# Turning the adjacency blocks on VectorE in 32 x 32 blocks, squaring on ScalarE, and partial mixes that stay in their banks

## The reference

```python
h = maximum(layernorm(x), 0)
msg = h @ W0 + B
weights = where(adj < 1, exp(-(1/adj - 1)**2 / (2 * 0.5**2)), 0)   # 0 where adj is 0
x = x + weights @ msg                                             # first layer

h = maximum(layernorm(x), 0)
A = adj + eye
d = sum(A, axis=1) ** -0.5
x = x + relu(d[:, None] * A * d[None, :] @ (h @ W1.T))             # second layer
```

## Time and profile before

| what | value |
|---|---|
| median of 3 runs | 651.94 us (651.78 to 652.38) |
| span of the profiled execution | 651.7 us |
| PE busy | 595.8 us, 91% |
| DVE busy | 523.2 us, 80% |
| ACT busy | 479.0 us, 73% |
| moved by DMA | 157.67 MB, mean 242 GB/s |

### The profile page before, as it was taken

One profiled execution on the slowest core, in us unless ns is written; L12 is line 12 of the kernel. 1 busy time (PEld: TensorE's weight loads), 2 busy tenths in 40 slices (PEclk: granted clock), 3 DMA queues, 4 the chain that ended last, 5 costly groups with the idle time before them and its releaser, 6 DMA issues.

```text
span 651.7 us, 7163 instructions
## 1 busy us (share of the span) xinstructions
PE 595.8 (91%) x2307; PEld 337.1 (52%) x2307; DVE 523.2 (80%) x582; ACT 479.0 (73%) x357; POOL 65.2 (10%) x87
## 2 busy tenths in 40 slices
PE   2498988977979999999999999999999999999995
PEld 2475644544545555655555555554555554444432
DVE  4999999999999999999999994668763868531516
ACT  2799999999999999999999986476484665710000
POOL 2694000000000100010001000100000000001110
PEclk9799999999999999999999999999999999999999
DMA  9987685797886778677678883585744550527983
GB/s 258 388 322 252 236 293 194 263 313 261 271 284 229 253 264 303 252 237 266 223 272 312 300 337 130 186 283 194 268 168 152 202 221 0 205 83 301 301 295 104
DMA packets 54293, 157.67 MB, mean 242 GB/s; under 512 B 2561, under 2 KB 11010, under 8 KB 43778
## 3 DMA queue, kind: packets, MB, share of 16 engines
q1 hardware_dynamic: 48370, 114.43, 50.8%
q0 software_dynamic: 5904, 42.99, 18.0%
HBM read 112.33 MB, written 45.09 MB: 242 GB/s over the span
## 4 chain that ended last, share of the span: by engine, by line
PE 58%; DVE 22%; ACT 8%; issue 8%; DMA 3%; DVEq 0%; SPq 0%; ACTq 0%; POOL 0%; POOLq 0%
PE acc L381 18%; PE acc_late L420 11%; PE acc_once L397 11%; PE turned_ps L364 9%; PE turned_ps L519 6%; DVE rowpart L659 6%; DVE wt L680 5%; DVE wt L673 4%; DMA late<-adj_t_spill 3%; ACT wt L586 2%; PE side L420 2%; ACT wt L580 2%; ACT kept L569 2%; ACT wt L574 2%; DVE msg L779 1%
## 5 line engine op out<-in xcount | busy, mean ns | idle before, releaser
L381 PE MATMUL acc<-wt,msg 128*128 128x512 f32 x512 | 231.8, 596 | 20.4 <-ACT wt L586 20.4
L569 ACT COPY kept<-turned_ps 128x1024 f32<-128x1024 f32 x128 | 124.0, 1027 | 75.5 <-PE turned_ps L364 73.6
L680 DVE SCALAR_TENSOR_TENSOR wt<-wt 128x2048 f32<-128x2048 f32 x64 | 146.3, 2286 | 20.8 <-ACT wt L580 20.7
L381 PEld LDWEIGHTS acc<-wt,msg 128*128 128x128 f32 x512 | 93.8, 190 | 126.9 <-issue 101.9
L659 DVE TENSOR_REDUCE rowpart<-raw 128x4 f32<-128x2048 f32 x64 | 145.8, 2278 | 7.7 <-DMA raw<-in_adj_dram 7.7
L673 DVE SCALAR_TENSOR_TENSOR wt<-kept 128x2048 f32<-128x2048 f32 x64 | 146.2, 2284 | 5.0 <-ACT kept L569 5.0
L364 PEld LDWEIGHTS turned_ps<-ident,raw 128*128 128x128 f32 x1024 | 119.8, 144 | 36.7 <-issue 29.8
L364 PE MATMUL turned_ps<-ident,raw 128*128 128x128 f32 x1024 | 126.9, 279 | 9.6 <-DMA raw<-in_adj_dram 9.4
L586 ACT ACTIVATE wt<-wt 128x2048 f32<-128x2048 f32 x64 | 123.2, 1926 | 15.7 <-DVE wt L680 15.7
L574 ACT ACTIVATE wt<-wt 128x2048 f32<-128x2048 f32 x64 | 124.3, 1943 | 0.1
L580 ACT ACTIVATE wt<-wt 128x2048 f32<-128x2048 f32 x64 | 122.8, 1919 | 0.0
(11 more groups left out here) (74 smaller groups left out, 216.2 us busy)
## 6 DMA issues: line engine op xcount, KB each, us to landing
raw<-in_adj_dram SPq DMA_DIRECT2D x64, 1024.0 KB, 5.7
adj_t_spill<-kept SPq DMA_DIRECT2D x41, 1024.0 KB, 7.1
late<-adj_t_spill POOLq DMA_DIRECT2D x41, 1024.0 KB, 5.3
x<-in_x_dram SPq DMA_DIRECT2D x4, 512.0 KB, 7.7
out_dram<-fin SPq DMA_DIRECT2D x8, 256.0 KB, 3.2
w_sb<-in_L_gnn_W_dram SPq DMA_DIRECT2D x2, 64.0 KB
b_row<-in_L_gnn_B_dram SPq DMA_DIRECT2D x1, 0.5 KB
```

Of the source, the lines that this page charges most:

```text
L381: mm = nc.tensor.matmul(acc0[:], msg[:, c * T + q, :], wt[:, p % WTS, q, :], start=(p % G == 0 and q == 0), stop=(p % G == G - 1 and q == ...
L569: nc.scalar.copy(kept[:, p % KEPT, q:q + 2, :], turned_ps[:, q:q + 2, :]).then_inc(copied, 1)
L680: nc.vector.scalar_tensor_tensor(out=v, in0=v, scalar=-2.0, in1=v, op0=ALU.add, op1=ALU.mult).then_inc(quad_done, 1)
```

## The change

A block is now called a unit, u = 0 to 63; row g has units 8g to 8g + 7. A load covers a pair of units (512 rows, 1024 columns): 2 MB in a layout in which partition 32q + i holds, for each of 16 groups e of 64 rows (32 of which belong to this half h), row i of the group and the 256 columns of quarter q. DVE's 32 x 32 block transpose of this layout has the column index on the partitions at once. Index lists of rows and columns follow the order that this gives (`by_tile`, `in_tiles`).

```diff
-G = 8
-ORDER = [1, 3, 4, 0, 7, 2, 5, 6]
-RAW, KEPT, WTS = 4, 4, 4
-MUL_LAG = 3
+RAW, KEPT, WTS, LATE = 2, 4, 6, 3
+LAG = 3
+ORDER = [[0, 1, 2, 3, 4, 5, 6, 7]]
+for turn_row in range(1, G):
+    young = turn_row - 1
+    ORDER.append([c for c in range(G) if c // 2 != young // 2] + [young ^ 1, young])
+JOBS = {17: [(0, 0)], 25: [(0, 1)], 28: [(1, 1)],
+        33: [(0, 2)], 35: [(1, 2)], 38: [(2, 2)],
+        41: [(0, 3)], 43: [(1, 3)], 45: [(2, 3)], 47: [(3, 3)],
+        48: [(0, 4)], 49: [(1, 4)], 51: [(2, 4)], 53: [(3, 4)], 55: [(4, 4)],
+        56: [(1, 5)], 57: [(2, 5)], 59: [(3, 5)], 61: [(4, 5)], 63: [(5, 5)]}
+TAIL = [(2, 6), (3, 6), (4, 6), (5, 6), (6, 6), (0, 5), (0, 6), (1, 6),
+        (2, 7), (3, 7), (4, 7), (5, 7), (6, 7), (7, 7), (0, 7), (1, 7)]
...
+        mix = [ps(f"mix{i}", [D, ROWS]) for i in range(6)]
+        once_bank = mix + mix[0:2]
+        tail_bank = [acc0, side] + mix[2:] + mix[0:2]
+        adj_parts = adj.rearrange("(R e h i) (C q w) -> R h C q i e w", e=16, h=2, i=B, C=C4, q=Q)
...
# SP
+            def load(n):
+                g = n // C4
+                if n >= RAW:
+                    sp.wait_ge(summed, n - RAW + 1)
+                    sp.wait_ge(turned, 2 * (n - RAW + 1))
+                for q in range(Q):
+                    sp.dma_start(raw[q * B:(q + 1) * B, n % RAW],
+                                 adj_parts[g // 2, g % 2, col(2 * n) // 2, q]).then_inc(raw_loaded[n % RAW], 16)
...
+            load_x(0)
+            load(0)
...
+            for u in range(UNITS):
+                if spills(u):
+                    sp.wait_ge(turned, u + 1)
+                    store(u)
+                if u % 2 == 1 and u // 2 + RAW < PAIRS:
+                    load(u // 2 + RAW)
...
# PE
+            for u in range(UNITS):
+                g, idx = u // G, u % G
+                if g == 0 and idx % 2 == 0:
+                    turn_h0(idx // 2)
+                    multiply_msg(idx // 2)
+                if g >= 1 and idx == 1:
+                    sum_quads(g - 1)
+                if at_once(u) and idx < G - 1 and not (g >= 6 and idx == 0):
+                    mix_once(u)
+                if g >= 1 and idx == 4:
+                    turn_x1(g - 1)
+                if u >= LAG:
+                    multiply_weights(u - LAG)
+                if g >= 1 and idx == 6:
+                    multiply_support(g - 1)
+                for i, (r, c) in enumerate(JOBS.get(u, [])):
+                    mix_late(first_job(u) + i, mix[r], r == 0 and c == 0, (r, c) in ((0, 4), (1, 5)))
+                if g >= 6 and idx == 0:
+                    mix_once(u)
+                if g >= 1 and idx == 5:
+                    turn_hid(g - 1)
+                if g >= 1 and idx == G - 1:
+                    mix_once(u)
...
# ACT
+            def square(u):
+                v = wt[:, u % WTS]
+                act.wait_ge(inv_done, u + 1)
+                nc.scalar.activation(v, v, ACT.Square, bias=-1.0).then_inc(square_done, 1)
...
+            def evict(r):
+                act.wait_ge(late_done, IN_TURN.index((r, r + 4)) + 1)
+                nc.scalar.copy(mixed[:, r], mix[r][:]).then_inc(evicted, 1)
...
+            for u in range(UNITS):
+                g, idx = u // G, u % G
+                log(u)
+                if u >= 1:
+                    square(u - 1)
+                if g >= 1 and idx == 6:
+                    log_pows(g - 1)
+                invert(u)
+                if u >= 1:
+                    weigh(u - 1)
+                if g == 0 and idx in (1, 3, 5):
+                    std_rows((idx + 1) // 2)
+                    copy_h0((idx + 1) // 2)
+                if g >= 1 and idx == 3:
+                    copy_x1t(g - 1)
+                if g >= 6 and idx == 0:
+                    evict(g - 6)
+                if g >= 1 and idx == 6:
+                    exp_pows(g - 1)
+                    copy_hid(g - 1)
...
# DVE
+            def turn(u):
+                n, h = u // 2, col(u) % 2
+                if u % 2 == 0:
+                    dve.wait_ge(raw_loaded[n % RAW], 64 * (n // RAW + 1))
+                if u >= KEPT:
+                    v = u - KEPT
+                    if spills(v):
+                        dve.wait_ge(spilled[v % KEPT], 16 * spill_count(v))
+                    if at_once(v):
+                        dve.wait_ge(once_done, once_count(v))
+                dst = kept[:, u % KEPT].rearrange("p k (e i) -> p e k i", i=B)
+                src = raw[:, n % RAW].rearrange("p e (k h i) -> p e k h i", k=T, h=2)[:, :, :, h, :]
+                nc.vector.transpose(dst, src).then_inc(turned, 1)
+
+            def row_sum(n):
...
+                nc.vector.tensor_reduce(dst, src, AX_X, ALU.add).then_inc(summed, 1)
+
+            def cut(u):
...
+                if u >= WTS:
+                    dve.wait_ge(acc0_done, u - WTS + 1)
...
+            take_moments(0)
+            for u in range(UNITS):
+                g, idx = u // G, u % G
+                turn(u)
+                if g == 0:
+                    cut(u)
+                if idx % 2 == 1:
+                    row_sum(u // 2)
+                if g == 0 and idx % 2 == 0:
+                    invert_std(idx // 2)
+                    if idx < 6:
+                        take_moments(idx // 2 + 1)
+                    if idx == 2:
+                        make_quads()
+                elif g == 0:
+                    make_msg(idx // 2)
+                if g >= 1 and idx == 2:
+                    own_rows(g - 1)
+                if g >= 1 and idx == 5:
+                    make_x1(g - 1)
+                if g >= 1 and idx == 7:
+                    make_support(g - 1)
+                if g >= 1:
+                    cut(u)
```

More of the change, by code:

```diff
@@ L83 @@
[L83 to L97, removed]
+C4 = 4
+Q = 4
+B = 32
+T = 4
+RAW, KEPT, WTS, LATE = 2, 4, 6, 3
@@ L401, in mix_late, with turn_h0 @@
[L401 to L422 removed]
+            def turn_h0(c):
+                pe.wait_ge(h0_done, c + 1)
+                if c >= 1:
+                    pe.wait_ge(h0_t_done, c)
+                for a in range(8):
+                    last = nc.tensor.transpose(turn_bank[a // 4][:, (a % 4) * P:(a % 4 + 1) * P],
+                                               support[:, c * 8 + a, :], ident[:])
+                last.then_inc(h0_turned, 1)
@@ new lines, in mix_once @@
+            def mix_once(u):
+                g, c = u // G, col(u)
+                pe.wait_ge(turned, u + 1)
+                if c == g - 1:
+                    pe.wait_ge(sup_done, g)
+                first = [v for v in range(g * G, g * G + G) if at_once(v)][0] == u
+                if first and g >= 6:
+                    pe.wait_ge(evicted, g - 5)
+                for k in range(T):
+                    mm = nc.tensor.matmul(once_bank[g][:], support[:, c * T + k, :], kept[:, u % KEPT, k, :],
+                                          start=(first and k == 0), stop=False)
+                mm.then_inc(once_done, 1)
@@ L536, in _ @@
[L536 to L552 removed]
+            ended = 0
@@ new lines, in _ @@
+            loads = len(IN_TURN)
+            for t, (r, c) in enumerate(TAIL):
+                if t == 0:
+                    sum_quads(G - 1)
+                if t < LAG:
+                    multiply_weights(UNITS - LAG + t)
+                if t == 4:
+                    turn_x1(G - 1)
+                if t == 5:
+                    turn_hid(G - 1)
+                if t == 6:
+                    multiply_support(G - 1)
+                if (r, c) == (1, 6):
+                    pe.wait_ge(sup_done, G)
+                if c == G - 1 and r == 2:
+                    pe.wait_ge(sup_done, G)
+                if (r, c) == (G - 1, G - 1):
+                    for k in range(T):
+                        mm = nc.tensor.matmul(tail_bank[r][:], support[:, c * T + k, :],
+                                              kept[:, (UNITS - 2) % KEPT, k, :], start=False, stop=(k == T - 1))
+                    mm.then_inc(late_done, 1)
+                else:
+                    mix_late(loads, tail_bank[r], (r, c) in ((0, 5), (1, 6)), c == G - 1)
+                    loads += 1
+                if c == G - 1:
+                    ended += 1
+                    if ended >= 2:
+                        turn_out(ended - 2)
@@ new lines, in _, with finish @@
+            own_rows(G - 1)
+            make_x1(G - 1)
+            make_support(G - 1)
+            def finish(i):
+                r = ENDS[i]
+                rows = slice(r * T, r * T + T)
+                dve.wait_ge(mix_turned, i + 1)
+                if i >= 2:
+                    dve.wait_ge(out_written[i % 2], 64 * (i // 2))
+                nc.vector.tensor_tensor(fin[i % 2], tail_bank[r][:].rearrange("p (a d) -> p a d", a=T),
+                                        support[:, rows, :], ALU.add).then_inc(out_summed, 1)
+                dve.wait_ge(out_summed, i + 1)
+                for a in range(T):
```

(1 more changed line is left out.)

804 lines of the change are left out of this document (303 added, 501 removed), and 6 rows, old and new, of the table LATE.

## The result

The changed kernel took **678.30 us** (median of 4, 675.93 to 678.89), the kernel before beside it 651.86 (4 runs, 651.69 to 652.38). The ratio is 1.040 with a 95% interval of 1.038 to 1.042: 4% slower, where 644 was forecast.

The account below looks back on a forecast made before the run. VectorE and ScalarE were taken as level, so queue orders decide. Start 11.1, first row 75.4, 58.3 to the first copy_hid end, light rows 255.3, heavy 71.9 and 75.3, tail 89.6: 636.9; plus 4 cold clock, 3 late adj: 644 us, range 622 to 672.

Parts of the forecast that it names:

- A wait that every row gets: Row from one copy_hid end to the next: 63.7 us, VectorE delivering cut 5' at 47.7, ScalarE wanting it at 48.4.
- Start: Before the first row, until 0.5 MB of x and 2.1 MB of adj land: 0.9 + 5.5 + 4.7 = 11.1 us.
- The estimate that the prediction set beside its sum: Loads of 32 partitions at 217 GB/s: 2 MB in about 14 us, start 4 us later, sum some 648.
- The prices of transpose, row sum and Square: New operations on VectorE and ScalarE: transpose 2.20 us, row sum of 4096 4.3, Square 1.80.
- the first row: First row of units, VectorE bound: 75.4 us.
- the wait at t0: At copy_hid's end, ScalarE idles 4.65 us for cut 7 behind make_support; cold support matmuls add 0.8 in light rows.
- the tail: From the last copy_hid end to the end of the span, mostly PE's remaining groups: 89.6 us.
- Rows 6 and 7: PE-heavy rows: PE waits for ScalarE's eviction, about 5 us, then turns x1t late; rows take 71.9 and 75.3 us.
- 1, the loads: Loads set the pace: a pair takes 22.8 us, 6.8 late at unit 4', deciding from 16; 678 us; chance 0.13.
- 2, the transpose at double cost: VectorE's block transpose costs twice, its row grows by 17 us: 728 us; chance 0.07.
- 3, half clock: PE at half clock in rows 1 to 3, own_rows holds VectorE 9 us: 668 us; chance 0.12.
- 4: Heavy rows don't wait for turn_x1, PE being further on: minus 19, 625 us; chance 0.13.

Follow-up runs that it names:

- experiment 1: Changed kernel with turn_x1 one unit earlier on PE, ahead of the row's first weight group: 643.03 us, ratio 0.986 to the kernel before.
- experiment 9: Kernel before with each 1 MB load of adj as four DMAs of 32 partitions, 2 KB runs: 656.51 us, ratio 1.006.
- experiment 10: Kernel before with each 1 MB load of adj as two DMAs of 128 partitions and 256 columns, 1 KB runs: 652.16 us, ratio 1.000.
- experiments 5 and 6: Changed kernel with the first two pairs' loads split over SyncE's and ScalarE's queues: 678.49 us; the same with turn_x1, cut 7 and make_quads also moved earlier: 628.08 us.
- experiment 11: Experiment 7 with each pair of units loaded in sixteen DMAs over all 128 partitions instead of four over 32: 975.59 us, ratio 1.495.
- experiment 7: Changed kernel with turn_x1 ahead of the weight group, cut 7 ahead of make_support, make_quads ahead of take_moments, one load queue: 626.47 us, ratio 0.959.

## Why the prediction was wrong

**The step that failed** is in "A wait that every row gets", the hand-over "cut 4' 35.9, row sum 42.4, `make_x1` 45.5, cut 5' 47.7 ... 0.7 us to spare". It let `make_x1` begin when VectorE was free, and took PE's `turn_x1` for ready. It followed PE's queue for the rows where PE is heavy and not for those where it is light. There PE idles, but in front of the weight group that waits for the same copy of `x1t` (the accumulator must be read before it is started anew), and in program order this group comes first. It took 5.2 to 6.3 us in rows 1 to 4, with a granted clock of 0.57 to 0.71 on average over the group, for 3.4 at full clock; in rows 4 and 5 a late job stands behind it too, as PE's timeline shows for row 4:

```profile
335.77 5.16 PE L350 MATMUL acc<-wt,msg 128*128 128x512 f32 x8 [11.32 <-ACT x1t L515]
340.77 3.60 PE L372 MATMUL mix<-late,support 128*128 128x512 f32 x8
344.20 0.60 PE L388 MATMUL side<-ident,x1t 128*128 128x128 f32 x4
```

That is far more than the 0.7 to spare. With the order mended (experiment 1) the rows are 63.5 to 64.5 us apart, where the prediction had 63.7: the rest of that paragraph was right.

**Start.** Forecast 11.1, measured 17.6. Two sizes were off. The sum let adj be issued from 0.9 us on; SyncE issues the eight loads of x first, 3.7 us, as its own row shows:

```profile
0.73 3.69 SPq L262 DMA_DIRECT2D x<-in_x_dram  x8
4.47 2.05 SPq L256 DMA_DIRECT2D raw<-in_adj_dram  x4
```

and the rate from 4 to 16 us was 167 to 225 GB/s, not 336. Two of the windows:

```profile
8.00:12.00 4.00, 0.00 (x0) 0.00 (x0) 2.06 (x14) 0.00 (x0) 0.00 (x0) 1.00 1.11 225
12.00:16.00 4.00, 0.00 (x0) 0.00 (x0) 0.00 (x0) 0.00 (x0) 0.00 (x0) 1.00 1.14 205
```

The estimate that the prediction set beside its sum, by the port rule of the Trainium skill (SBUF — State Buffer, section Door 1), had the rate; the sum went by whole megabytes.

**What was right.** The prices of transpose, row sum and Square; the first row, though partly by luck: its transposes and cuts took 1.2 more than forecast, Newton steps and `make_msg` 1.1 less, and 16 x 2.20 + 4 x 4.3 is 52.4 where the sum has 52.6; the wait at t0 (5.60 in each light row, forecast 4.65 and 0.8 for cold support matmuls, measured 2.08 for 1.05); the tail. Rows 6 and 7 are 2.2 and 1.2 off, but by another way. The count of PE's groups left out the late jobs of units 47 and 55, which stand behind t0: five groups, not four, come before the evicted bank. So PE waited for the eviction under 1 us, not 5, and `turn_x1` began 53.0 and 55.4 us after t0, for a forecast of 50.6 and 54.1. Two errors of near 4 us cancelled there.

**The rivals.** 1, the loads: its time, 678, was met by chance. A part took 10.5 us from issue to landing (median) where the rival's point of decision was 16 for a pair, but several are in flight, and adj held up VectorE 9.0 us in all, 7.5 of it at the start. 2, the transpose at double cost: no. 3, half clock: its places were right in part (0.50 ahead of the weight group, and `own_rows`' wait came only in rows 6, 7 and the tail, 15.2 us in three), its price was not. 4: no. No case of mine held one group in the way of another on PE in the light rows, so the range of 622 to 672 was too narrow on the side where each queue's order had not been followed.

## What to carry to other kernels

When two engines are level and the order of the queues decides, write out every engine's queue between the two hand-overs, the light engine's too: an idle engine isn't at hand, it stands in front of its next instruction, and if that waits for the same event as yours, its time comes first, at the clock that idling left. Put the small operation that another engine waits for ahead of the large one that nobody waits for. A change that took 86 us of work off an engine came out 26 us slower by such places, and 4% faster (626.5 against 652) once two calls on PE, two on VectorE and the constants had changed places.

## What the runs showed of the hardware

- A block transpose (32 x 32) of 128 x 2048 f32 from a strided layout takes 2305 ns, as any other full VectorE pass here.
- One group of four f32 matmuls 128 x 128 by 128 x 512 (x8 in the trace) took 6.31 us with a granted clock of 0.50 through its first 5 us, and 3.67 at 1.00.
- Loads in parts of 32 partitions moved at 219 and 225 GB/s with 2 KB runs (experiment 9, 16 to 24 us), loads over 128 partitions at 348 with 1 KB runs (experiment 10, 16 to 20 us).
- With parts of the lower and of the upper 64 partitions in flight from two queues, the rate was 289 and 298 GB/s from 13 to 14 us (experiments 5 and 6), against 210 and 214 with lower parts alone two microseconds later; it had been some 205 in the first 0.7 us with both.
- Loads whose source has a slowest dimension of 4 kept some four DMA engines busy (share 0.27), and experiment 11 took 1.56 times as long as experiment 7, which loads the same bytes in as many packets.
- SyncE took 0.46 us to issue one 64 KB load at the start (3.69 for 8).
